# Edge products of a graph layer: from 64-row fp32 to 128-row fp32r with stacked high and low parts

## The chip, the cores and the metric

The kernel runs on one NeuronCore of a Trainium2 chip. The metric is the device time of one execution in microseconds (us). A second kind of execution is profiled: it gives a span (first to last instruction) and the trace from which all rows below are copied.

## The reference, cut to what matters

```
src, dst = edge_index                      # 131072 edges, sorted by dst; 8192 nodes, 256 channels
ea  = edge_attr @ w_e + b_e                # (131072, 64) @ (64, 256)
msg = relu(x[src] + ea)
agg = segment_sum(msg, dst, 8192)
t   = x + agg
h_local = bn1(relu(t @ w1 + b1) @ w2 + b2 + x)
# 32 blocks of 256 nodes, attention with 4 heads inside graphs of 32 nodes
h_attn  = bn2(softmax(q k^T / 8) v @ out_w.T + out_b + x)
out = h_local + h_attn
out = bn3(out + relu(out @ m_w1 + m_b1) @ m_w2 + m_b2)
return layernorm(x + out)
```

All of it is in fp32. The part that changes is the first product, `edge_attr @ w_e`.

## The kernel before, in words

**Tiles.** The edges are cut into 128 groups of 1024 edges, a group into 8 tiles of 128 edges, and two tiles make a pair: 512 pairs. A pair fills one PSUM bank of 128x512 values (128 edges, twice 256 channels). Four banks `EA[0..3]` take the pairs in turn.

**Turns.** All engines run one list of turns, written out by hand, each engine in its own program order with semaphores between them. A turn handles two pairs: turn t works on pairs 2t and 2t+1, so 256 turns carry edges and 19 more finish the nodes. A group is two turns. For one pair:

- GpSimd (POOL) issues two indirect DMAs (line 304), one per tile, which fetch the rows `x[src]` into one of 8 slots `xg`. It may be 8 pairs ahead of the engine that empties the slots.
- The pair's bank is seeded with these rows. For pairs 0 to 79 (`XB_PAIR` = 80) VectorE adds `b_e` while it seeds (`seed`, line 442). For the others `b_e` is in the rows already: VectorE adds it to all of `x` in 16 parts (`XB`) during the first turns (`add_be`, line 541), SyncE stores each part to `xb_dram`, and the later gathers read from there. ScalarE then only copies (`seed`, line 330). Seeds are made one turn ahead of the product.
- TensorE adds the edge product on top of the seed (`products`, line 707): for the two pairs of a turn four fp32 products of 64 rows. The edge attributes `ea` of one pair lie in SBUF partitions 0 to 63 and those of the other in 64 to 127, the weights `we` are there twice, so two such products use the two halves of the array at once.
- ScalarE takes the relu and rounds it to fp32r (`mh`, line 334), VectorE computes what the rounding lost (`ml`, `low`, line 533), and once per group TensorE sums both by destination with 16 fp32r products of a one-hot matrix (line 722). VectorE makes the one-hot (line 545). ScalarE copies the sum (line 339), TensorE transposes it (line 731), VectorE adds it to `aggT` (line 563).

**Nodes.** Every 8 turns a block of 256 nodes goes through attention (16 steps) and another through the layers behind it (13 steps, `node`), spread over the turns between the edge work; line 677 is the helper that issues most of their fp32 products.

**Order on the queues that the change touches.** SyncE loads `ea` into three buffers (line 201), two groups ahead of use, and waits for the product before it reuses a buffer. In every odd turn up to 31 it waits for `add_be` of a part, stores that part (line 242) and loads the next one (line 231); the parts have two buffers `xrow`. On VectorE a turn reads: seeds, then in even turns `add_agg`, `add_be` and the one-hot, then the two `low`, then attention and node steps. On ScalarE: seeds, the two `high`, in odd turns the copy of the sum, then attention and node steps.

## Time and profile before

| | us |
|---|---|
| median of three runs | 1360.22 (1359.91 to 1360.58) |
| the profiled execution | 1364.96 |
| its span | 1363.1 |
| TensorE busy | 1270.4 (93%) |
| VectorE busy | 904.9 (66%) |
| ScalarE busy | 751.6 (55%) |
| GpSimd busy | 987.6 (72%) |
| TensorE's granted clock, mean over the span | 0.979 of full speed |

Busy is a union over the span and says nothing about waits: an instruction stream can be without a gap in its issue and still show 72%. The profiled execution is longer than the median run by 4.7 us, and its span lies 1.9 us below its own time. The rows come from that one execution.

### The profile page before, as it was taken

How to read it: one execution, taken by the hardware profiler on the slowest of the kernel's cores; microseconds unless marked ns; L12 is line 12 of the kernel's file. 1: busy time of each engine (PE TensorE's matmuls, PEld its weight loads, DVE VectorE, ACT ScalarE, POOL GpSimd, SP SyncE). 2: the span in 40 equal slices, each digit the busy share in tenths (PEclk: the TensorE clock that was granted, in tenths of full speed). 3: DMA queues.
4: the chain of work that ended last, by engine and by line, in shares of the span. 5: the costliest groups of instructions: out<-in, count | busy, mean ns of one | idle time of the engine just before them, and what ended most of it. 6: DMA issues, size and time to landing. Idle time of an engine off the chain costs nothing.

```text
span 1363.1 us, 22611 instructions
## 1 busy us (share of the span) xinstructions
PE 1270.4 (93%) x8250; PEld 1024.2 (75%) x8250; DVE 904.9 (66%) x1763; ACT 751.6 (55%) x1617; POOL 987.6 (72%) x1032
## 2 busy tenths in 40 slices
PE   3787889999999999999999999999999999999997
PEld 2666678887877777777778777777877777778786
DVE  4988987666666665667666566666666666556652
ACT  1333335665665656566665666666656656565642
POOL 7777777777777777777777777777777777777710
PEclk6889999999999999999999999999999999999999
DMA  9777765555555554555555555555555555545511
GB/s 328 236 242 244 243 212 157 172 151 164 160 174 174 160 174 139 174 161 176 174 159 163 148 166 170 174 164 172 149 161 160 175 177 160 172 131 167 153 52 47
DMA packets 109648, 232.89 MB, mean 171 GB/s; under 512 B 21984, under 2 KB 46816, under 8 KB 109536
## 3 DMA queue, kind: packets, MB, share of 16 engines
q0 software_dynamic: 49152, 134.28, 34.1%
q1 hardware_dynamic: 58944, 93.87, 20.6%
q10 hardware_dynamic: 1440, 3.29, 0.6%
q8 instruction: 65, 1.06, 0.3%
q14 instruction: 47, 0.39, 0.1%
HBM read 206.19 MB, written 25.17 MB: 170 GB/s over the span
## 4 chain that ended last, share of the span: by engine, by line
POOL 35%; PE 23%; DMA 15%; issue 13%; ACT 7%; DVE 6%; SPq 0%; DVEq 0%; ACTq 0%
POOL xg L304 35%; DMA xg<-xb_dram,srcs 12%; PE both L677 8%; PE bank L722 4%; PE bank L707 4%; ACT bank L330 3%; PE bank L677 3%; ACT mh L334 2%; DVE onehot L545 1%; DMA aggT<-in_xT_dram 1%; DVE ml L533 1%; PE bank L731 1%; PE both L853 1%; DMA xg<-in_x_dram,srcs 1%; PE bank L800 1%
## 5 line engine op out<-in xcount | busy, mean ns | idle before, releaser
L304 POOL DMA_INDIRECT xg<-xb_dram,srcs x864 | 819.3, 948 | 263.2 <-issue 227.0
L330 ACT COPY bank<-xg 128x512 f32<-128x512 f32 x432 | 256.3, 598 | 373.5 <-DMA xg<-xb_dram,srcs 341.7
L533 DVE SCALAR_TENSOR_TENSOR ml<-bank,mh 128x512 fp32r<-128x512 f32 x512 | 328.6, 683 | 154.6 <-ACT mh L334 153.6
L334 ACT ACTIVATE mh<-bank 128x512 fp32r<-128x512 f32 x512 | 276.7, 593 | 137.6 <-PE bank L707 136.4
L707 PE MATMUL bank<-we,ea 64*128 64x256 f32 x2048 | 296.1, 409 | 56.7 <-DVE bank L442 28.3
L707 PEld LDWEIGHTS bank<-we,ea 64*128 64x128 f32 x2048 | 181.7, 191 | 139.1 <-issue 68.3
L722 PE MATMUL bank<-mh,onehot 128*128 128x256 f32 x1024 | 265.8, 297 | 8.3 <-DVE onehot L545 8.2
L722 PE MATMUL bank<-ml,onehot 128*128 128x256 f32 x1024 | 252.3, 284 | 0.0
L722 PEld LDWEIGHTS bank<-mh,onehot 128*128 128x128 f32 x1024 | 196.4, 192 | 51.8 <-issue 29.5
L304 POOL DMA_INDIRECT xg<-in_x_dram,srcs x160 | 167.3, 1046 | 50.8 <-issue 46.9
L722 PEld LDWEIGHTS bank<-ml,onehot 128*128 128x128 f32 x1024 | 197.1, 192 | 0.0
L563 DVE TENSOR_TENSOR aggT<-bank,aggT 128x256 f32 x128 | 54.3, 424 | 159.2 <-PE bank L731 157.5
L545 DVE TENSOR_TENSOR onehot<-bank,rel 128x1024 fp32r<-128x1024 f32 x128 | 155.4, 1214 | 0.0
L677 PE MATMUL both<-xT,iwT 128*128 128x256 f32 x512 | 124.3, 386 | 0.0
L677 PE MATMUL both<-m,h 128*128 128x256 f32 x496 | 117.5, 380 | 1.0 <-ACT h L343 1.0
L677 PEld LDWEIGHTS both<-xT,iwT 128*128 128x128 f32 x512 | 92.1, 190 | 15.2 <-issue 5.3
L677 PEld LDWEIGHTS both<-m,h 128*128 128x128 f32 x496 | 89.4, 190 | 11.2 <-issue 1.4
L339 ACT COPY agg<-bank 128x256 f32<-128x256 f32 x128 | 47.7, 373 | 54.3 <-PE bank L722 54.2
L677 PE MATMUL both<-iwT,xT 128*128 128x256 f32 x256 | 68.3, 390 | 0.3 <-DVE dif L578 0.3
L677 PE MATMUL bank<-oT,owT 128*128 128x256 f32 x256 | 65.8, 379 | 0.8 <-ACT oT L367 0.8
L677 PE MATMUL bank<-h,w 128*128 128x256 f32 x256 | 65.7, 379 | 0.0
L677 PE MATMUL bank<-o,m 128*128 128x256 f32 x264 | 62.4, 379 | 1.0 <-DVE o L606 1.0
(100 smaller groups left out, 1368.3 us busy)
## 6 DMA issues: line engine op xcount, KB each, us to landing
ea<-in_ea_dram SPq DMA_DIRECT2D x128, 256.0 KB, 5.0
xg<-xb_dram,srcs POOLq DMA_INDIRECT x864, 3.0
xT<-in_xT_dram SPq DMA_DIRECT2D x32, 256.0 KB, 3.2
aggT<-in_xT_dram SPq DMA_DIRECT2D x32, 256.0 KB, 3.9
xrow<-in_x_dram SPq DMA_DIRECT2D x16, 512.0 KB, 6.1
xb_dram<-xrow SPq DMA_DIRECT2D x16, 512.0 KB, 3.7
oT_dram<-oT SPq DMA_DIRECT2D x32, 256.0 KB, 2.3
xn<-in_x_dram SPq DMA_DIRECT2D x32, 256.0 KB, 4.5
```

Source lines behind the costliest of these rows:

```text
L304: pool.indirect_dma_start(xg[:, q % NX, n * C:(n + 1) * C], None, t["x"] if q < XB_PAIR else k.xb_dram[:, :], bass.IndirectOffsetOnAxis(k. ...
L330: nc.scalar.copy(EA[q % 4][:, :], xg[:, q % NX, :]).then_inc(s_seed, 1)
L334: nc.scalar.activation(mh[:, q % NM, :], EA[q % 4][:, :], ACT.Relu).then_inc(s_mh, 1)
L339: nc.scalar.copy(k.agg[:, :], G[:, 0:C]).then_inc(s_agg, 1)
L533: nc.vector.scalar_tensor_tensor(ml[:, q % NM, :], EA[q % 4][:, :], 0.0, mh[:, q % NM, :].bitcast(fp32), ALU.max, ALU.subtract).then_inc(s ...
L545: nc.vector.tensor_tensor(onehot[:, n % 2, :, :], G[:, 2 * P:3 * P].unsqueeze(1).to_broadcast([P, TG, P]), k.rel[:, n, :].unsqueeze(2).to_ ...
L563: nc.vector.tensor_tensor(window, G[:, 0:C].rearrange("p (c n) -> p c n", n=P), window, ALU.add).then_inc(s_added, 1)
L677: ins = nc.tensor.matmul(to, stationary(c), moving(c), start=start and c == 0, stop=stop and c == blocks - 1)
L707: ins = nc.tensor.matmul(EA[(2 * d + pair) % 4][:, two * C:(two + 1) * C], ea[rows, n % NEA, at:at + P], k.we[rows, :], start=False, stop= ...
L722: ins = nc.tensor.matmul(G[:, 0:C], onehot[:, n % 2, tile, :], half[:, q % NM, two * C:(two + 1) * C], start=tile == 0 and half is mh, sto ...
L731: ins = nc.tensor.transpose(G[:, c * P:(c + 1) * P], k.agg[:, c * P:(c + 1) * P], ident[:, :])
L800: ins = nc.tensor.matmul(X[1][at:at + DH, col:col + P], k.vn[:, b, h * DH:(h + 1) * DH], k.probT[:, H * (h % 2) + 2 * b + h // 2, :], star ...
```

## The change

Each 128x512 tile of edge attributes is split into a high part (rounded to fp32r) and a low part (what the rounding lost), and the two are stacked over 128 partitions in a new tile `eahl`: for the first pair of a product high in partitions 0 to 63 and low in 64 to 127, for the second the other way round. The weights are split the same way (`weh`, `wel`). A turn then has 8 fp32r products of 128 rows, each with 256 columns, in place of four fp32 products of 64 rows.

The split is made once per group, in odd turns. ScalarE writes the rounded tile into a bank of pairs (`EA[2]`, free between `low` of its pair and its next seed), and copies the two 64-partition halves rounded into `eahl`; VectorE subtracts the bank from `ea` in two instructions of 64x512. ScalarE's split stands behind a wait for `low` of the turn's first pair, and its copy of the group sum (`copy_agg`) now stands behind that wait too. The next seed of the bank waits for VectorE's split.

The table with `b_e` is made in 32 parts of half the size, one in every turn up to 31, and not in 16. `XB_PAIR` stays at 80. `ea` has two buffers, not three, and is loaded one turn earlier relative to its split. In the attention `ex` and `prob` now share the memory of `dif`.

```diff
-NEA = 3
+NEA = 2
-XB = 16
+XB = 32
-XB_PAIR = XB * PG + 16
+XB_PAIR = 2 * XB + 16
...
@@ sync
             def load_ea(n):
                 if n >= NEA:
-                    sp.wait_ge(s_prod, 2 * (n - NEA) + 2)
+                    sp.wait_ge(s_eah, n - NEA + 1)
+                    sp.wait_ge(s_eal, n - NEA + 1)
...
-                if turn % 2 == 1 and turn // 2 + 2 < NG:
-                    load_ea(turn // 2 + 2)
-                m = turn // 2
-                if turn % 2 == 1 and m < XB:
+                if turn == 0:
+                    load_ea(2)
+                if turn % 2 == 0 and turn // 2 + 3 < NG:
+                    load_ea(turn // 2 + 3)
+                m = turn
+                if m < XB:
                     sp.wait_ge(s_xadd, m + 1)
                     sp.dma_start(xb_parts[m, :, :, :], k.xrow[:, m % 2, :, :]
                                  ).then_inc(s_xbst[m % 2], 16)
-                if turn % 2 == 1 and 2 <= m + 1 < XB:
+                if 2 <= m + 1 < XB:
                     load_part(m + 1)
@@ scalar
+                if q % 4 == 2 and q // 4 + 2 <= NG:
+                    act.wait_ge(s_eal, q // 4 + 2)
                 nc.scalar.copy(EA[q % 4][:, :], xg[:, q % NX, :]).then_inc(s_seed, 1)
...
+            def round_ea(n, bank):
+                act.wait_ge(s_ea[n % NEA], 16 * (n // NEA + 1))
+                nc.scalar.copy(bank[:, :].bitcast(f32r), ea[:, n % NEA, :]).then_inc(s_eab, 1)
+
+            def high_ea(n):
+                nc.scalar.copy(eahl[0:ED, n % 2, 0, :], ea[0:ED, n % NEA, :])
+                nc.scalar.copy(eahl[ED:P, n % 2, 1, :], ea[ED:P, n % NEA, :]).then_inc(s_eah, 1)
...
+                n = (turn + 3) // 2
+                if turn % 2 == 1 and n < NG:
+                    act.wait_ge(s_ml, a + 1)
+                    round_ea(n, EA[a % 4])
                 if turn % 2 == 1 and 3 <= turn <= 2 * NG + 1:
                     copy_agg(turn // 2 - 1)
-                n = turn // 2 + 1
-                if turn % 2 == 0 and EA_PE <= n < NG:
-                    act.wait_ge(s_ea[n % NEA], 16 * (n // NEA + 1))
+                if turn % 2 == 1 and n < NG:
+                    high_ea(n)
@@ vector
+            def low_ea(n, bank):
+                dve.wait_ge(s_eab, n + 1)
+                nc.vector.tensor_tensor(eahl[ED:P, n % 2, 0, :], ea[0:ED, n % NEA, :],
+                                        bank[0:ED, :], ALU.subtract)
+                nc.vector.tensor_tensor(eahl[0:ED, n % 2, 1, :], ea[ED:P, n % NEA, :],
+                                        bank[ED:P, :], ALU.subtract).then_inc(s_eal, 1)
...
-                    if n < XB:
-                        add_be(n)
                     if n < NG:
                         make_onehot(n)
+                if 1 <= turn < XB:
+                    add_be(turn)
                 for q in (a, b):
                     if q < NP:
                         low(q)
+                if turn % 2 == 1 and (turn + 3) // 2 < NG:
+                    low_ea((turn + 3) // 2, EA[a % 4])
@@ tensor, products
-                for two in range(2):
-                    for pair in range(2):
-                        rows = slice(pair * ED, (pair + 1) * ED)
-                        ins = nc.tensor.matmul(EA[(2 * d + pair) % 4][:, two * C:(two + 1) * C],
-                                               ea[rows, n % NEA, at:at + P], k.we[rows, :],
+                for pair in range(2):
+                    for two in range(2):
+                        for half in (k.weh, k.wel):
+                            ins = nc.tensor.matmul(EA[(2 * d + pair) % 4][:, two * C:(two + 1) * C],
+                                                   eahl[:, n % 2, pair, at:at + P], half[:, :],
```

On VectorE, two turns of the first thirty (an odd and an even one) read in the kernel before like this; `ml<-bank,mh` is `low`, `bank<-be_rows,xg` is `seed`:

```order
L442 TENSOR_TENSOR bank<-be_rows,xg 128x512 x2
L533 SCALAR_TENSOR_TENSOR ml<-bank,mh 128x512 x2
L442 TENSOR_TENSOR bank<-be_rows,xg 128x512 x2
L552 TENSOR_LOAD base_i
L552 ISA x2
L563 ISA
L563 TENSOR_TENSOR aggT<-bank,aggT 128x2x128
L541 TENSOR_TENSOR xrow<-be_rows,xrow 128x1024
L545 TENSOR_TENSOR onehot<-bank,rel 128x1024
L533 SCALAR_TENSOR_TENSOR ml<-bank,mh 128x512 x2
```

and in the changed kernel like this (`eahl<-ea,bank` is `low_ea`):

```order
L473 TENSOR_TENSOR bank<-be_rows,xg 128x512 x2
L583 TENSOR_TENSOR xrow<-be_rows,xrow 128x512
L575 SCALAR_TENSOR_TENSOR ml<-bank,mh 128x512 x2
L481 TENSOR_TENSOR eahl<-ea,bank 64x512
L483 TENSOR_TENSOR eahl<-ea,bank 64x512
L473 TENSOR_TENSOR bank<-be_rows,xg 128x512 x2
L594 TENSOR_LOAD base_i
L594 ISA x2
L605 ISA
L605 TENSOR_TENSOR aggT<-bank,aggT 128x2x128
L587 TENSOR_TENSOR onehot<-bank,rel 128x1024
L583 TENSOR_TENSOR xrow<-be_rows,xrow 128x512
```

Two instructions of 64x512 come into every odd turn, `add_be` stands in both turns with half the length, and in the even one it has moved behind the one-hot.

On SyncE's queue, four turns of the same part of the program before:

```order
L242 DMA xb_dram<-xrow 128x1024
L231 DMA xrow<-in_x_dram 128x1024
L201 DMA ea<-in_ea_dram 128x512
L242 DMA xb_dram<-xrow 128x1024
L231 DMA xrow<-in_x_dram 128x1024
```

and in the changed kernel:

```order
L208 DMA ea<-in_ea_dram 128x512
L251 DMA xb_dram<-xrow 128x512
L238 DMA xrow<-in_x_dram 128x512
L251 DMA xb_dram<-xrow 128x512
L238 DMA xrow<-in_x_dram 128x512
L208 DMA ea<-in_ea_dram 128x512
```

A store and a load of a part now stand in every turn. The load of part m+1 stands, as before, behind the store of part m, which waits for `add_be` of part m; between that wait and `add_be` of part m+1 lies one turn, where two lay before.

## Rows read from the trace of the kernel before

**Rows 1.** What engines waited for over the whole span: us in total, times, longest.

```profile
ACT bank L330 <- DMA xg<-xb_dram,srcs: 341.7, 213, 4.5
POOL xg L304 <- issue: 273.9, 899, 0.3
...
POOL xg L304 <- DVE bank L442: 2.4, 5, 1.2
```

**Rows 2.** The page's part 5: gathers (busy, mean ns | idle before).

```profile
L304 POOL DMA_INDIRECT xg<-xb_dram,srcs x864 | 819.3, 948 | 263.2 <-issue 227.0
...
L304 POOL DMA_INDIRECT xg<-in_x_dram,srcs x160 | 167.3, 1046 | 50.8 <-issue 46.9
```

**Rows 3.** Windows by engine, busy us (instructions), PEclk, DMA share, GB/s.

```profile
27.20:97.80 70.60, 54.85 (x330) 42.30 (x332) 63.83 (x111) 21.43 (x45) 54.41 (x51) 0.80 0.73 240
97.80:183.20 85.40, 72.25 (x478) 57.33 (x478) 77.11 (x132) 30.58 (x68) 66.25 (x63) 0.98 0.75 241
...
400.00:600.00 200.00, 194.37 (x1281) 156.72 (x1280) 129.09 (x256) 123.08 (x266) 151.35 (x160) 1.00 0.55 165
```

**Rows 4.** Timeline in steady state: start, us, engine, instruction [idle before <-releaser].

```profile
606.76 1.13 PE L707 MATMUL bank<-we,ea 64*128 64x256 f32 x8
...
607.83 0.39 PE L722 MATMUL bank<-mh,onehot 128*128 128x256 f32 x1
...
609.72 0.28 PE L722 MATMUL bank<-ml,onehot 128*128 128x256 f32 x1
```

**Rows 5.** Groups by line, whole span, of VectorE and ScalarE.

```profile
L533 DVE SCALAR_TENSOR_TENSOR ml<-bank,mh 128x512 fp32r<-128x512 f32 x512 | 328.6, 683 | 154.6 <-ACT mh L334 153.6
...
L330 ACT COPY bank<-xg 128x512 f32<-128x512 f32 x432 | 256.3, 598 | 373.5 <-DMA xg<-xb_dram,srcs 341.7 <-DVE ml L533 29.1
...
L442 DVE TENSOR_TENSOR bank<-be_rows,xg 128x512 f32<-128x512 f32 x80 | 52.2, 693 | 12.9 <-DMA xg<-in_x_dram,srcs 12.7
...
L541 DVE TENSOR_TENSOR xrow<-be_rows,xrow 128x1024 f32<-128x1024 f32 x16 | 19.4, 1214 | 7.5 <-DMA xrow<-in_x_dram 7.5
```

**Rows 6.** Timeline of VectorE in the first turns.

```profile
97.78 1.23 DVE L541 TENSOR_TENSOR xrow<-be_rows,xrow 128x1024 f32<-128x1024 f32 x1 [0.42 <-DMA xrow<-in_x_dram]
98.92 1.22 DVE L545 TENSOR_TENSOR onehot<-bank,rel 128x1024 fp32r<-128x1024 f32 x1
...
116.92 1.29 DVE L533 SCALAR_TENSOR_TENSOR ml<-bank,mh 128x512 fp32r<-128x512 f32 x2
118.13 1.29 DVE L442 TENSOR_TENSOR bank<-be_rows,xg 128x512 f32<-128x512 f32 x2
119.33 0.42 DVE L563 TENSOR_TENSOR aggT<-bank,aggT 128x256 f32 x1
```

**Rows 7.** Windows of line 304 alone: gathers issued.

```profile
0.00:183.20 183.20, 139.06 (x132) 0.87 0.77 256
```

**Rows 8.** Windows of line 442 alone: seeds made.

```profile
0.00:183.20 183.20, 41.91 (x64) 0.87 0.77 256
```

**Rows 9.** DMA issues in 27.2 to 183.2: count, KB, median us to landing.

```profile
xb_dram<-xrow SPq DMA_DIRECT2D x15, 512.0 KB, 3.7
xrow<-in_x_dram SPq DMA_DIRECT2D x14, 512.0 KB, 6.1
ea<-in_ea_dram SPq DMA_DIRECT2D x15, 256.0 KB, 6.0
...
oT_dram<-oT SPq DMA_DIRECT2D x3, 256.0 KB, 2.0
```

**Rows 10.** The same view in 400 to 600.

```profile
xT<-in_xT_dram SPq DMA_DIRECT2D x5, 256.0 KB, 3.3
```

**Rows 11.** The chain of waits in the first 50 us: start, us, what.

```profile
21.11 6.03 DMA xrow<-in_x_dram
```

**Rows 12.** Timeline of GpSimd in the first turns.

```profile
98.05 1.78 POOL L304 DMA_INDIRECT xg<-in_x_dram,srcs  x1 [0.30 <-issue]
```

**Rows 13.** Timeline of TensorE near the end.

```profile
1273.83 2.08 PE L707 MATMUL bank<-we,ea 64*128 64x256 f32 x8 [2.60 <-ACT bank L330]
```

More of the change, by code:

```diff
@@ L95, in gnn_layer @@
         k.rel = sb("rel", [P, NG, TG])
-        k.we = sb("we", [P, C])
+        k.weh, k.wel = sb("weh", [P, C], f32r), sb("wel", [P, C], f32r)
         k.be_rows = sb("be_rows", [P, C])
@@ L122, in gnn_layer @@
         k.dst_p = k.oT[:, :, :, :].rearrange("p a c (g t) -> p (a c g) t", t=TG).bitcast(i32)
+        k.we = k.qT[:, 0, :]
         k.gammas = k.xn[:, :, :, :].rearrange("p a b c -> p (a b) c")[:, 0:3, :]
@@ L160, in program @@
         s_oh = sem("s_onehot_made")
+        s_weh, s_wel = sem("s_we_high"), sem("s_we_low")
+        s_eab, s_eah, s_eal = (sem(n) for n in ("s_ea_high_in_bank", "s_ea_high", "s_ea_low"))
         s_pre = [sem(f"s_agg_preloaded_{n}") for n in range(2)]
@@ L401, in node @@
                                          ).then_inc(s_root, 1)
+            act.wait_ge(s_we, 16)
+            nc.scalar.copy(k.weh[:, :], k.we[:, :]).then_inc(s_weh, 1)
+            for n in range(2):
+                round_ea(n, X[1 + n])
+                high_ea(n)
             for turn in range(TURNS):
@@ L441, in seed @@
                     dve.wait_ge(s_ml, q - 3)
+                if q % 4 == 2 and q >= 6:
+                    dve.wait_ge(s_eal, q // 4 + 2)
                 nc.vector.tensor_tensor(
@@ L455, in _ @@
             seed(1)
+            dve.wait_ge(s_weh, 1)
+            nc.vector.tensor_tensor(k.wel[:, :], k.we[:, :], k.weh[:, :].bitcast(fp32),
+                                    ALU.subtract).then_inc(s_wel, 1)
+            low_ea(0, X[1])
             dve.wait_ge(s_dstg, 16)
@@ L643, in node @@
                     ins.then_inc(s_y, 1)
+            low_ea(1, X[2])
             add_be(0)
@@ L690, in _ @@
                                 ).then_inc(s_baseT, 1)
-            pe.wait_ge(s_we, 16)
+            pe.wait_ge(s_wel, 1)
             def products(d):
                 n, h = d // 2, d % 2
-                if h == 0 and n < EA_PE:
-                    pe.wait_ge(s_ea[n % NEA], 16 * (n // NEA + 1))
+                if h == 0 and n < 2:
+                    pe.wait_ge(s_eah, n + 1)
+                    pe.wait_ge(s_eal, n + 1)
                 if 2 * d < XB_PAIR:
```

17 lines of the change are left out of this document (8 added, 9 removed).

## The prediction

> **What bounds the kernel now.** I read the waits first. GpSimd never waits for anybody for long: before nearly every gather it sits idle 0.3 us on its own issue, and in the whole span it waits 2.4 us for VectorE's seeds [rows 1]. ScalarE, in contrast, waits 341.7 us for gathered rows, and TensorE, busy 97% of a steady stretch, still gets its pauses from late seeds [rows 1, 3, 13]. So the stream of gathers sets the pace, although the page calls GpSimd 72% busy. Its price: (819.3 + 263.2) / 864 = 1.253 us for one late gather, (167.3 + 50.8) / 160 = 1.363 us for one of the first 160 [rows 2]. Four gathers make a turn: 5.01 us later, 5.45 us in the first 40 turns.
>
> The first gathers are slower because some are stretched from 0.95 us to as much as 1.78 us, and these lie beside `add_be` and the seeds of VectorE, which read two SBUF operands: the 1.78 us gather at 98.05 runs beside the `add_be` at 97.78 [rows 6, 12]. The Trainium skill says the same in GPSIMD Engine Reference, Key points: GpSimd contends with VectorE instructions that have two SBUF inputs. By that rule the new `low_ea`, one operand of which is in PSUM, stretches nothing; `low`, which reads PSUM too, runs all through the stretch 400 to 600, where 160 gathers were busy 151.35 us, 0.946 us each [rows 3, 5].
>
> Then I look at who is close behind GpSimd, by stretch. From 400 to 600 VectorE is busy 129.09 of 200 us and ScalarE 123.08. From 27.2 to 183.2, which is turns 0 to 30 (turn 30 has made seeds number 63 and 64 by 183.2), VectorE is busy 63.83 + 77.11 = 140.9 of 156.0 us, 90% [rows 3, 8]. A turn takes 5.20 us there. At 183.2 GpSimd has issued 132 gathers, 66 pairs, against 64 pairs seeded [rows 7, 8]: it is 2 pairs ahead where the slots allow 8. That unused lead decides what a slower VectorE costs.
>
> **TensorE.** Products before: from the start of one to the next instruction on TensorE 607.83 - 606.76 = 1.07 us [rows 4]. The new ones have the form of the one-hot sums: fp32r, 128 rows, 256 columns. Sixteen of these start from 607.83 to 609.72, 0.126 us apart [rows 4]. Eight make 1.01 us, or 0.95 us if the first longer step is not paid. I take a gain of 0.1 us a turn. Bounds: none, and, if a gap of 64-row work at both ends of the products goes, 0.3 us. Because GpSimd sets the pace it counts only where TensorE is the chain, from the last wait for a seed at 1273.83 to the end [rows 13]: some 7 turns with products, -1 us.
>
> The Trainium skill, TensorEngine Tiling (Array Packing), Key Properties, says that a change of tiling mode drains TensorE. The 1.07 us would leave 0.1 us for it, but no row isolates the drain. If the rule alone were right and TensorE the bound, the change would be worth the gain of every turn; that is the last rival.
>
> **ScalarE.** It adds per group one copy into PSUM (598 ns as line 330's) and two copies of 64x512. For the last two no row exists; length along the free dimension is that of line 330, so I take 0.6 us; bounds 0.37 us and 0.7 us [rows 5]. Sum 1.8 us per group, 0.9 us a turn, on an engine busy 123.08/200 x 5.01 = 3.1 us a turn: 4.0 of 5.01 us. In the first turns it is far from full. It costs nothing as throughput. As latency: in odd turns the next seeds stand behind the wait for `low`, the rounding, the copy of the sum and two more copies. Counted from the end of an odd turn's products that is 1.1 (two `high`) + 0.2 + 0.6 + 0.4 + 1.1 + about 1 of node work = 4.4 us and then 1.1 us of seeds, against more than 8 us until the product that needs them. The one tight place is a short turn behind an attention step, where eight instructions of 256 elements (8 x 0.42 = 3.4 us, by the 128x256 one at 119.33) stand ahead of `low` on VectorE; I estimate a stall up to 0.5 us per 8 turns, inside the 5.6 us that TensorE is idle in 200 us [rows 3] plus the 4 us that it gains. So: nothing.
>
> **VectorE.** `low_ea` is two instructions of 64x512 with a PSUM operand per group. The row nearest is `low`: 683 ns, two in 118.13 - 116.92 = 1.21 us, 0.60 us each in a stream [rows 5, 6]. Bounds 0.42 us (the 128x256 instruction at 119.33) and 0.69 us. That is 0.60 us a turn. `add_be`: 1.14 us before per two turns (97.78 to 98.92), now two of the seeds' size, 1.20 us: +0.03 a turn. The first `low_ea` waits a little for ScalarE's bank: +0.07. Sum +0.70 us a turn.
>
> Behind turn 32 this is covered (0.65 + 129.09/200 x 5.01 = 3.9 of 5.01 us). In turns 0 to 30 the cover is 10%. Pace without gathers: (156.0 - 3)/30 + 0.70 = 5.80 us; the 3 us are my estimate of what VectorE waited there for gathers, out of the 12.7 us in all [rows 5]. If all its idle time there vanished, 140.9/30 + 0.70 = 5.40 us. What GpSimd tolerates: the gather of pair 66 needs pair 58 seeded, the work of turn 28, by 183.2. The first part now has 256 KB, not 512, and its load landed at 27.14 [rows 11]; I let it land 2.5 us sooner, so turn 0 starts at 24.7 and the limit is (183.2 - 24.7)/28 = 5.66 us a turn. At 5.80 turn 28 comes at 187.1: 3.9 us late, and four more turns against GpSimd's 85.40/63 x 4 = 5.42 us add 1.5. Together +5.4 us. Bounds: 0 (5.40) and +10.
>
> **SyncE and the parts.** Before, between `add_be` of part m and that of part m+1 there were two turns; the load landed after 6.1 us at the median and only 0.42 us was waited for one at 97.78 [rows 6, 9]. Now it is one turn, and the load is issued behind the store, 0.40 us after `add_be`. From an even turn's `add_be` to the next one VectorE has two `low` and two seeds, 2.4 us, plus the attention or node steps of that turn (about 3 us in two of four cases, none to 1.3 in the other two, counted at 0.42 us an instruction). From an odd one it has 2.4 + 1.2 + 0.35 + 1.14 = 5.1 us. Landing time of 256 KB: lower bound 3.3 us [rows 10], upper 6.0 [rows 9]. I take 4.0: a store of 256 KB lands in 2.0 (oT's row), and 512 KB behind a store of 512 KB land 6.1 + 0.4 - 3.7 = 2.8 us after it, so half needs 1.4, with 0.6 us for gathers and `ea` in between. Then 4.4 us are needed, and the bare turns wait 2.0 us, two in eight in turns 1 to 16, and 1.3 and 0.5 in the 16 behind them with node work: 8 + 3.6 = 11.6 us, of which some 4 lie in idle time counted already. +8 us. At 3.3 us: +2. At 6.0 us nearly every turn waits, some 14 us in eight turns: +50.
>
> **Sum.** The stages add: +5.4 + 8 (early) - 1 (end) - 1 (two half-length `add_be` hold off a gather for less time than one: squares of the lengths, 32 x 0.69^2 = 15 against 16 x 1.21^2 = 23, beside 67 for the 40 double seeds, of the 160 x 0.11 = 18 us that the first gathers are stretched) = +11 us. The profiled execution, span 1363.1 in 1364.96 us, would be 1376. The median of the runs stands 4.7 us under it; the difference carries over: 1360.2 + 11 = 1371 us.
>
> **Rivals.**
> - The lead covers it. VectorE's idle time shrinks, loads land in 3.3 us, the pace stays under 5.66 us. Then only savings are left: GpSimd's 1.2 us wait (the longest in rows 1) for a late first seed, 1.6 us less stretching, 1 us at the end: 1356.4, faster. For it: 6 unused pairs, worth 6 x 2.6 = 16 us. Against: VectorE at 90%. It decides from a pace below 5.66 us. With part of the delay left: up to 1363.
> - Latency in steady state. If ScalarE's order costs TensorE over 1.1 + 0.8 us in 8 turns (its idle time and gain there), TensorE with its waits becomes slower than 40.1 us in 8 turns. At 1.5 us over, 27 times, +40: 1400. For it: TensorE at 97%, with six steps put between `high` and the next seeds. Against: seeds a turn ahead, eight slots.
> - The parts' loads take 6 us: +50, with the +5 partly inside: about 1412.
> - TensorE is the bound after all: 256 x 0.11 = 28 us, 1332. Against it: GpSimd without a pause.
>
> **Chances.** Forecast 0.48 (its own range 1363.5 to 1390); covered 0.27, of it 0.12 faster and 0.15 the same; latency 0.14; slow loads 0.08; TensorE 0.03. A measurement of this kernel can tell about 0.2%, 2.7 us. Faster 0.15, same 0.15, slower 0.70. The range 1357 to 1404 leaves out TensorE's case, the fastest end of the covered one, and the slow loads.
>
> **What would show it.** Right: gathers of line 304 among the first 160 that wait for the seed by VectorE, tens of us and not 2.4; VectorE over 93% busy from 25 to 200 us and turn 30 at some 205 us, not 183; waits of `add_be` for `xrow`, 5 to 15 us in all; from 400 to 600 still 160 gathers; eight products at 0.12 us steps. Wrong: gathers fewer than 160 in that stretch (latency), no wait of GpSimd in the first 200 us (covered), or a last gather at 1302 with an end elsewhere.

## The result, and the profile after

The changed kernel takes 1390.67 us (median of 4 runs, 1387.56 to 1392.12), the kernel before 1360.31 us (4 runs, 1359.91 to 1360.58): 1.022 times as long, interval 1.0203 to 1.0238, +30.4 us. The forecast was 1371, +11, with a range of 1357 to 1404. Its direction and the place of the loss hold; its size is a third of what came. The step that failed is the sum for VectorE's early stage, +13.4 us with the parts' loads, where the runs show 26.0: VectorE fell behind faster, above all by its waits for the parts, and the gathers' lead took up less of it.

| | before | after |
|---|---|---|
| span of the profiled execution, us | 1363.1 | 1389.1 |
| first 160 gathers, busy + idle, us | 218.1 | 242.3 |
| other 864 gathers, busy + idle, us | 1082.5 | 1083.7 |
| start of the last gather, us | 1301.58 | 1326.87 |
| from there to the end of the span, us | 61.5 | 62.2 |
| seeds of turn 32 start, us | 192.73 | 225.82 |
| first gather from the finished table, us | 220.27 | 246.23 |

The groups of gathers after (busy, mean ns of one | idle before) come first, to be held against [rows 2]:

```profile
L313 POOL DMA_INDIRECT xg<-xb_dram,srcs x864 | 818.6, 947 | 265.1 <-issue 241.0 <-ACT bank L341 22.0 <-DVE bank L473 2.1
L313 POOL DMA_INDIRECT xg<-in_x_dram,srcs x160 | 161.0, 1006 | 81.3 <-issue 42.7 <-DVE bank L473 37.1 <-DMA srcs<-in_srcs_dram 1.5
```

Of the 26.0 us between the spans, 24.2 lie in the first 160 gathers, and there in idle time alone, 81.3 against 50.8 us; the gathers themselves became shorter. Another 1.8 us are the idle time in front of the 161st gather (2.09 against 0.30 us), which still waits for a seed of VectorE. The rest of the kernel adds nothing. What ended the idle time stands in the waits (total us, times, longest), which answer to [rows 1]:

```profile
POOL xg L313 <- issue: 283.7, 931, 0.3
ACT bank L352 <- DVE ml L575: 212.7, 126, 6.5
...
POOL xg L313 <- DVE bank L473: 39.2, 20, 3.5
PE both L722 <- ACT h L364: 38.5, 30, 1.6
...
DVE xrow L583 <- DMA xrow<-in_x_dram: 19.0, 9, 3.5
```

GpSimd waits for VectorE's seeds 39.2 us in 20 pieces, where it waited 2.4. ScalarE no longer waits for gathered rows (341.7 us before); its longest waits are now in front of the copy of line 352 (`round_ea`), which needs `low` to be done with the bank. The waits of GpSimd in its timeline (start, us, instruction, idle before it):

```profile
30.04 1.14 POOL L313 DMA_INDIRECT xg<-in_x_dram,srcs  x1 [1.31 <-DVE bank L473]
...
71.41 1.15 POOL L313 DMA_INDIRECT xg<-in_x_dram,srcs  x1 [3.21 <-DVE bank L473]
...
120.20 1.14 POOL L313 DMA_INDIRECT xg<-in_x_dram,srcs  x1 [3.47 <-DVE bank L473]
...
246.23 0.94 POOL L313 DMA_INDIRECT xg<-xb_dram,srcs  x1 [2.09 <-DVE bank L473]
```

They run from the first turn to the 161st gather, 246.23, and there is none of this size behind it. The windows by engine, PE, PEld, DVE, ACT, POOL (instructions), show both stages, to be held against [rows 3]:

```profile
27.20:225.80 198.60, 142.05 (x851) 124.92 (x852) 175.72 (x306) 80.91 (x165) 129.94 (x128) 0.86 0.67 208
400.00:600.00 200.00, 187.92 (x1290) 172.22 (x1289) 158.17 (x297) 159.71 (x329) 151.23 (x161) 1.00 0.57 166
```

From 400 to 600 there are 161 gathers in 151.23 us, as before (160 in 151.35), although VectorE and ScalarE are now busy 158 and 160 of 200 us. But the chain of work that ended last, in part 4 of the page, no longer runs through them. Before it read:

```profile
POOL 35%; PE 23%; DMA 15%; issue 13%; ACT 7%; DVE 6%; SPq 0%; DVEq 0%; ACTq 0%
```

and after:

```profile
PE 45%; DVE 32%; ACT 13%; DMA 4%; issue 3%; DVEq 1%; SPq 0%; ACTq 0%
```

No seed that ScalarE makes waits for its rows any more. ScalarE starts the seed of pair 144 (counted from 0) at 422.31 us and that of pair 464 at 1216.85, which is 4.97 us a turn, where the gathers take 5.01. So behind the table TensorE, VectorE and ScalarE run at a pace of their own, only 0.04 us a turn faster than the gathers. This small margin matters for the size of the loss. The 161st gather waits for the first seed of turn 35. Before, VectorE started it at 209.55, and the gather started 10.0 us after the seed's end:

```profile
209.55 1.29 DVE L442 TENSOR_TENSOR bank<-be_rows,xg 128x512 f32<-128x512 f32 x2
...
220.27 1.47 POOL L304 DMA_INDIRECT xg<-xb_dram,srcs  x1 [0.30 <-issue]
```

In the changed kernel VectorE comes to it 35.2 us later:

```profile
244.75 1.29 DVE L473 TENSOR_TENSOR bank<-be_rows,xg 128x512 f32<-128x512 f32 x2
```

and the gather starts at 246.23, 26.0 us later than before. The lead of the gathers took up 9.2 us of VectorE's lateness, and the engines behind them make these 9 us good at 0.04 us a turn over the 220 turns that are left. By this reckoning the kernel would have ended up to 9 us later without that margin.

In the first stretch VectorE is busy 175.72 of 198.6 us. Its timeline shows what fills a turn there:

```profile
95.49 0.69 DVE L583 TENSOR_TENSOR xrow<-be_rows,xrow 128x512 f32<-128x512 f32 x1 [1.79 <-DMA xrow<-in_x_dram]
96.10 1.28 DVE L575 SCALAR_TENSOR_TENSOR ml<-bank,mh 128x512 fp32r<-128x512 f32 x2
97.44 0.68 DVE L481 TENSOR_TENSOR eahl<-ea,bank 64x512 fp32r<-64x512 f32 x1
98.14 0.69 DVE L483 TENSOR_TENSOR eahl<-ea,bank 64x512 fp32r<-64x512 f32 x1
98.96 1.30 DVE L473 TENSOR_TENSOR bank<-be_rows,xg 128x512 f32<-128x512 f32 x2
```

The `add_be` at 95.49 sits idle 1.79 us for its part. The second `low` starts some 0.6 us after the first and would be followed at about 97.30; the first low half starts at 97.44, and from there to the seeds are 98.96 - 97.44 = 1.52 us. With the 0.14 us before it, `low_ea` takes 1.66 us of these two turns. The chain of waits (start, us, what) shows where the part was late:

```profile
41.24 0.61 DVE xrow L583
41.85 0.02 issue
41.86 0.33 SPq L251
...
42.23 5.12 DMA xrow<-in_x_dram
...
47.38 0.69 DVE xrow L583
```

It is a ring: `add_be` lets SyncE store the part (0.33 us of issue), the next load goes out behind the store, at 42.23, and the following `add_be` starts as the load lands, 5.12 us later. With 16 parts the ring had two turns for one round, with 32 it has one.

On TensorE the eight products (start and duration, us) went as forecast:

```profile
602.14 0.36 PE L753 MATMUL bank<-weh,eahl 128*128 128x256 f32 x1
602.34 0.28 PE L753 MATMUL bank<-wel,eahl 128*128 128x256 f32 x1
602.46 0.28 PE L753 MATMUL bank<-weh,eahl 128*128 128x256 f32 x1
...
603.18 0.28 PE L767 MATMUL bank<-mh,onehot 128*128 128x256 f32 x1
```

From the first product to the next instruction are 603.18 - 602.14 = 1.04 us, 1.07 before [rows 4]. Its busy time from 400 to 600 fell from 194.37 to 187.92 us, and the gathers' pace didn't change with it.

### The profile page after: what moved, and what is told of

It is laid out like the page before. It is cut to its first block, busy times and chain, and to the rows that moved or that the text cites. A ratio compares the mean times of both kernels' runs of the same rounds, so it can differ in the third digit from the quotient of the medians.

```text
span 1389.1 us, 23482 instructions
## 1 busy us (share of the span) xinstructions
PE 1234.5 (89%) x8250; PEld 1123.0 (81%) x8250; DVE 1088.4 (78%) x2036; ACT 973.5 (70%) x2002; POOL 980.6 (71%) x1032
## 4 chain that ended last, share of the span: by engine, by line
PE 45%; DVE 32%; ACT 13%; DMA 4%; issue 3%; DVEq 1%; SPq 0%; ACTq 0%
PE both L722 16%; DVE ml L575 9%; PE bank L722 8%; PE bank L767 8%; PE bank L753 8%; DVE probT L637 4%; DVE dif L620 4%; DVE mx L616 4%; DVE onehot L587 4%; DMA xrow<-in_x_dram 3%; ACT bank L352 3%; ACT eahl L356 2%; PE bank L845 2%; ACT bank L341 2%; ACT eahl L355 2%
## 5 line engine op out<-in xcount | busy, mean ns | idle before, releaser
L753 PE MATMUL bank<-weh,eahl 128*128 128x256 f32 x1024 | 302.3, 327 | 26.6 <-DVE bank L473 26.6
L341 ACT COPY bank<-xg 128x512 f32<-128x512 f32 x432 | 245.2, 601 | 31.1 <-DVE ml L575 29.5
L753 PE MATMUL bank<-wel,eahl 128*128 128x256 f32 x1024 | 260.9, 286 | 0.0
L767 PE MATMUL bank<-mh,onehot 128*128 128x256 f32 x1024 | 257.8, 288 | 1.1 <-DVE onehot L587 1.1
L753 PEld LDWEIGHTS bank<-weh,eahl 128*128 128x128 f32 x1024 | 198.7, 194 | 40.7 <-DVE bank L473 31.3
L352 ACT CAST bank<-ea 128x512 fp32r<-128x512 f32 x127 | 75.0, 590 | 212.7 <-DVE ml L575 212.7
L313 POOL DMA_INDIRECT xg<-in_x_dram,srcs x160 | 161.0, 1006 | 81.3 <-issue 42.7
L753 PEld LDWEIGHTS bank<-wel,eahl 128*128 128x128 f32 x1024 | 199.7, 195 | 4.6
L776 PE MATMUL bank<-ident,agg 128*128 128x128 f32 x256 | 51.6, 284 | 51.7 <-ACT agg L360 51.7
L481 DVE TENSOR_TENSOR eahl<-ea,bank 64x512 fp32r<-64x512 f32 x127 | 86.5, 681 | 7.6
L483 DVE TENSOR_TENSOR eahl<-ea,bank 64x512 fp32r<-64x512 f32 x127 | 87.6, 690 | 1.8
```

The costliest lines, as they stand in the source:

```text
L313: pool.indirect_dma_start(xg[:, q % NX, n * C:(n + 1) * C], None, t["x"] if q < XB_PAIR else k.xb_dram[:, :], bass.IndirectOffsetOnAxis(k. ...
L341: nc.scalar.copy(EA[q % 4][:, :], xg[:, q % NX, :]).then_inc(s_seed, 1)
L352: nc.scalar.copy(bank[:, :].bitcast(f32r), ea[:, n % NEA, :]).then_inc(s_eab, 1)
L481: nc.vector.tensor_tensor(eahl[ED:P, n % 2, 0, :], ea[0:ED, n % NEA, :], bank[0:ED, :], ALU.subtract)
L483: nc.vector.tensor_tensor(eahl[0:ED, n % 2, 1, :], ea[ED:P, n % NEA, :], bank[ED:P, :], ALU.subtract).then_inc(s_eal, 1)
L753: ins = nc.tensor.matmul(EA[(2 * d + pair) % 4][:, two * C:(two + 1) * C], eahl[:, n % 2, pair, at:at + P], half[:, :], start=False, stop= ...
```

## The experiments

A job is a set of runs made one after the other on one chip, the kernel before among them. Two kinds have to be told apart. In the jobs that ran the full-length variants, the kernel before itself took 1766 to 1800 us (medians); in the jobs with the lightened kernels (below) it took 1359 to 1360, as at first, and one chip showed both, in two jobs one after the other. In the long jobs the gathers don't set the pace:

```profile
400.00:600.00 200.00, 160.56 (x927) 126.54 (x927) 94.99 (x186) 90.89 (x191) 111.54 (x118) 0.90 0.42 124
```

This is the kernel before in such a job (the same columns as in the windows above): 118 gathers in 200 us instead of 160, and TensorE only 160.56 us busy. The waits of the same run:

```profile
ACT mh L334 <- remote: 443.7, 73, 13.7
POOL xg L304 <- ACT bank L330: 388.5, 110, 5.8
...
PEld bank L707 <- issue: 95.5, 210, 4.0
PEld bank L722 <- issue: 73.4, 131, 6.1
```

In the rows shown TensorE's weight loads pause for nothing that the profile shows, up to 6.1 us at once. Such rows stood in the first profile too, but smaller: 68.3 us in all on line 707 (the longest 4.0 as here), and 29.5 us with none over 0.3 on line 722. A wait whose releaser the profile can't name is "remote"; ScalarE has 443.7 us of them on one line, and had none. The granted clock is 0.90 in this stretch, against 1.00; whether that comes from the pauses or has a part in them isn't separated. A loss of 30 us in the stream of gathers can't be read there. The cause of these jobs is open.

**Full variants in long jobs.** Four edits, each run in two or more jobs. b32, the kernel before with the table in 32 parts alone:

```diff
-XB = 16
+XB = 32
...
-                if turn % 2 == 1 and m < XB:
+                if m < XB:
...
-                    if n < XB:
-                        add_be(n)
...
+                if 1 <= turn < XB:
+                    add_be(turn)
```

> The kernel before with one part of the change alone: the table in 32 parts of half the size, one add_be per turn, XB_PAIR still 80. Theory (VectorE's early work uses up the gathers' lead): about 15 us of add_be waiting for xrow as in the changed kernel, turn 32 at 205 to 212 us, which the lead of 6 unused pairs nearly covers: 1360 to 1366 us. Rival (the loads of the parts alone are the loss): 1375 us or more. Rival (the parts cost nothing, all loss is the split): 1359 to 1361 us with waits of add_be under 5 us.

> The same kernel as b32 (the 32 parts alone in the kernel before). Theory: about 15 us of add_be waiting for xrow, nearly covered by the gathers' lead: 1360 to 1366 us. Rival (the parts are the loss): 1375 us or more.

nosplit, the changed kernel without the split beyond groups 0 and 1 (the products take the old halves, so the edge part of the result is that of the first groups). The waits that belong to these calls go or are bounded with them:

```diff
-                    round_ea(n, EA[a % 4])
...
-                    high_ea(n)
...
-                    low_ea((turn + 3) // 2, EA[a % 4])
```

> The changed kernel with the split of the edge attributes left out for all groups but the first two (eahl keeps the first two groups' values, so the edge products are computed from those): TensorE's new products and the 32 parts remain, ScalarE and VectorE do none of the split. Theory: as b32 less at most 2 us, 1358 to 1365 us: TensorE's gain per turn buys nothing in the steady stretch, where still 160 gathers fall in 200 us, and ScalarE waits for gathers again. Rival (TensorE sets the pace): 1335 to 1345 us.

> The same kernel as nosplit (new products and parts, no split but for the first two groups, so the edge products use old values). Theory: 1358 to 1365 us, ScalarE waits for gathers again, 160 gathers in 400 to 600 us. Rival (TensorE sets the pace): 1335 to 1345 us.

nolow, the same with ScalarE's half of the split kept (only the low halves are the old ones); the seeds that waited for `low_ea` wait for `round_ea` instead:

```diff
-                if turn % 2 == 1 and (turn + 3) // 2 < NG:
-                    low_ea((turn + 3) // 2, EA[a % 4])
```

> The changed kernel with VectorE's half of the split (low_ea) left out for all groups but the first two; ScalarE's rounding into the bank and its two copies remain, with their places in the order. The low halves of the edge attributes keep old values. Theory: VectorE's early pace is that of b32, so 1358 to 1366 us, within 3 us of nosplit. Rival (ScalarE's order and latency cost in the steady stretch): most of the loss stays, 1380 us or more, with fewer than 160 gathers in 400 to 600 us.

> The same kernel as nolow (ScalarE's part of the split stays, VectorE's is left out but for the first two groups, so the low halves keep old values). Theory: within 3 us of nosplit, 1358 to 1366 us. Rival (ScalarE's order costs in the steady stretch): 1380 us or more; on the slow chip nolow was as slow as pf and 1.2% above nosplit, which speaks for this rival where TensorE is the bound.

pf, the changed kernel with the load of the next part ahead of SyncE's wait:

```diff
                 m = turn
+                if 2 <= m + 1 < XB:
+                    load_part(m + 1)
                 if m < XB:
                     sp.wait_ge(s_xadd, m + 1)
...
-                if 2 <= m + 1 < XB:
-                    load_part(m + 1)
```

> The changed kernel with SyncE's load of part m+1 issued ahead of its wait for add_be of part m (it waits only for the store of part m-1), nothing else changed. Theory: the 15.5 us of add_be waiting for xrow after turn 0 go almost whole, early pace 5.7 to 5.9 us a turn in place of 6.21, gathers wait 15 to 25 us for seeds in place of 39, 1374 to 1382 us. Rival (the split alone would be enough to use up the lead): 1385 to 1390 us, since VectorE then waits elsewhere. Rival (the parts' loads are the whole loss): 1360 to 1363 us.

> The same kernel as pf, for a comparison on a chip on which the kernel before takes 1360 us; on the chip of the first comparison it took 1766 us, TensorE paused between its own matmuls there and gathers waited for ScalarE, so that another bound was measured. Theory: 15 us less waiting of add_be for xrow, gathers wait 15 to 25 us for seeds, 1374 to 1382 us. Rival (the split alone uses up the lead): 1385 to 1390 us. Rival (the parts' loads are the whole loss): 1360 to 1363 us.

> The changed kernel with SyncE issuing the load of the table's part m+1 ahead of its wait for the sum of part m, so that VectorE no longer waits for a part in the early stage (19 us in the changed kernel, 3 us with this edit on the chip with TensorE's pauses). If this lands on a chip where the kernel before takes 1360 us. Theory (the loss is VectorE's pace past the lead): 10 to 16 us less than the changed kernel, so 1375 to 1381, 1.011 to 1.016 times the kernel before. Rival (the waits only cover time that VectorE would lose anyway, to late gathers): 1388 to 1391.

And both kernels themselves, with ib (run again as ib3): the kernel before with all seeds on ScalarE, and the bias added to the first 80 pairs by TensorE from its high and low parts (be2) with a constant 1/64, four products a turn:

```diff
+                            nc.tensor.matmul(EA[(2 * d + pair) % 4][:, two * C:(two + 1) * C],
+                                             k.frac[:, :], k.be2[:, :], start=False, stop=True,
+                                             skip_group_check=True)
```

> The kernel before, unchanged, for its trace on the chip at hand. If it takes 1360 us, the rows of the first trace again: 160 gathers in 400 to 600 us. If it takes 1766 us: about 120 gathers in 400 to 600 us, and idle time of TensorE in front of matmuls that wait for nothing, which would show that the gathers don't set the pace on that chip.

> The changed kernel itself, to have its ratio beside the others'. If the kernel before takes 1360 us here, 1.022 as before. If it takes about 1766 us, as on the chip of the two comparisons so far, no theory fixes the ratio: TensorE pauses between its own instructions there and the gathers are not the bound. If the loss is bound to the gathers' lead in the first 230 us, the ratio is the one of pf (1.013 to 1.015) within 0.4%; if the parts' late loads cost there too, 15 us or 0.9% more.

> The kernel before with the seeds of the first 80 pairs moved from VectorE to ScalarE (a plain copy, as for all later pairs) and b_e added on TensorE by one more fp32r product of 128 rows per tile (weights of 1/64, moving operand the high part of b_e in 64 rows and the low part in the other 64); the table, the parts and everything later as before. Theory: VectorE's 80 instructions with two SBUF operands were most of what stretched the first gathers, and VectorE's load of the first 40 turns falls by 1.2 us a turn, so where gathers set the pace the first 160 take about 205 us in place of 218, and the time is 1345 to 1350 us (0.99). Rival (the stretching comes from add_be, or from DMA traffic): 1358 to 1362 us. Where TensorE's own pauses set the pace: no change, or up to 19 us longer for 160 more products of 0.12 us.

> The kernel before with all seeds copied by ScalarE, and the bias of the edge rows added to the first 80 pairs' banks by TensorE (a 128-row product of a constant 1/64 with the bias' high and low parts): VectorE's reads of two SBUF operands per pair are gone and the gathers' mean is 0.97 us instead of 1.05 (measured on the chip with TensorE's pauses). If the kernel before takes 1360 us here. Theory (the first 160 gathers are worth what they take, one for one): 8 to 14 us less than the kernel before, 1346 to 1352, since ScalarE's seeds leave no wait of the gathers. Rival (ScalarE, with eight more columns of work a turn, or TensorE's 8 added products a turn, set the pace in their place): 1360 or more.

| | median us (times the kernel before, interval) |
|---|---|
| b32 | 1768.22 (1.0004, 0.9962 to 1.0045); 1770.19 (1.0011, 0.9983 to 1.0039) |
| nosplit | 1767.42 (1.0015, 0.9955 to 1.0075); 1770.79 (0.9997, 0.9968 to 1.0027) |
| nolow | 1789.79 (1.013, 1.0088 to 1.0173); 1786.14 (1.010, 1.0062 to 1.0138) |
| pf | 1789.51 (1.013, 1.0082 to 1.0178); 1790.44 (1.0149, 1.006 to 1.0238); 1795.29 (1.0121, 1.0052 to 1.019) |
| kernel after | 1804.5 (1.0042, 1.0004 to 1.0079) |
| kernel before, one run | 1803.34 |
| ib | 1802.07 (1.0004, 0.9965 to 1.0043); 1766.16 (1.0018, 0.9985 to 1.005) |

The times expected of b32, nosplit, nolow and pf, and most of those of ib, were for a kernel before of 1360 us, so these runs don't test them. before_here came as expected for a long job (118 gathers), and so did ib (no change). after_again didn't: the changed kernel costs 1.004 here, not 1.022, and less than the 1.013 to 1.015 of pf that were expected of it within 0.4%. nolow and pf, which leave out something of it, show 1.010 to 1.015 in other jobs, and nosplit and b32 show nothing; so in these jobs the cost goes with ScalarE's part of the split, perhaps, and not with VectorE's. With TensorE's pauses unexplained I don't build on that. Two rows of early turns can be used, since they are of one engine and its load. pf brought VectorE's wait for its parts down:

```profile
DVE xrow L583 <- DMA xrow<-in_x_dram: 3.0, 1, 3.0
```

And ib, without VectorE's reads of two SBUF operands in the seeds, has somewhat shorter gathers in the first 160:

```profile
L304 POOL DMA_INDIRECT xg<-in_x_dram,srcs x160 | 155.5, 972 | 115.3 <-ACT bank L333 63.7 <-issue 50.0 <-DMA srcs<-in_srcs_dram 1.6
```

972 ns is the mean (977 in ib3). It has to be held against the kernel before in the same job, which has 1003, and not against the 1046 of [rows 2]: the difference is 31 ns. Whether that is worth time where the gathers set the pace was not shown: both runs of ib fell into long jobs.

**Lightened kernels.** To take TensorE out of the question, four kernels and later a fifth leave out a part of its work, all in the same way: of each node-side product only the first block of the contraction is computed, the products with z are left out, and of the sums over a group the low halves.

```diff
-                for c in range(blocks):
...
+                for c in range(1):
...
-                    for half in (mh, ml):
+                    for half in (mh,):
```

The diff is cut; the products with z go in a third place. Waits, order and the other engines' work stay. light_before and light_after are the two kernels so lightened, light_b32, light_nolow and light_pf the variants above.

> The kernel before, with TensorE lightened: it leaves out every block but the first of the node side's products, the products with z, and the low halves in the sums over a group. On this chip the kernel before takes 1766 to 1803 us because TensorE pauses between its own matmuls; with some 0.9 us a turn less of them, by 1.25 us a gather the last of 1024 gathers should end at about 1300 and the kernel take 1350 to 1370 us. If the pauses grow with something else than the count of matmuls, it stays over 1600. Early stage as in the profile of the kernel before: some 145 gathers issued by 200 us.

> The changed kernel lightened in the same way. My theory (the loss is made in the first 160 gathers, by VectorE's turn of 6.2 us with the low halves and the 32 parts' loads): light_before plus 20 to 33 us, all of it in the first 160 gathers, whose busy and idle time together is some 24 us more than in light_before. Rival (the loss is made by the 128-row products or the bank lent for the split, over the whole kernel): the difference is spread over the 1024 gathers. Rival (the loss belongs to TensorE and is gone when it is lightened): within 3 us of light_before.

> light_before with the table in 32 parts alone (80 pairs seeded on VectorE as before). Theory: the loads of the parts make VectorE wait some 15 us in the first 160 gathers, but the lead of the gathers (16 us at turn 32) takes that up: light_before plus 0 to 4 us. Rival (the parts' loads alone are the loss): plus 15 to 20 us.

> light_after without VectorE's low halves beyond the first two groups (the low halves of those are used again): ScalarE's half of the split, the 128-row products and the 32 parts stay. Theory: VectorE's turn falls by 0.83 us, 32 turns of that are 27 us, so nearly all the loss is gone: light_before plus 0 to 6 us. Rival (loads, bank or products make it): light_before plus 15 us or more.

> light_after with the load of part m+1 issued ahead of SyncE's wait for the sum of part m. On a chip where the kernel before takes 1360 us: light_after is 1363.0 us and light_before 1338.0. Theory (the waits for the parts' loads are on VectorE's path once the lead is used up): VectorE's waits for xrow fall from 17 us to under 6, and the first 160 gathers' busy and idle time from 237.4 to some 225, so 1349 to 1355 us, near light_nolow's 1345. Rival (a wait gone is only replaced by a wait for a late gather): 1360 to 1364. On a chip with TensorE's pauses only the wait for xrow (under 6 us) can be read from it.

| | median us (runs) | over light_before | first 160 gathers, busy + idle, us | over light_before |
|---|---|---|---|---|
| light_before | 1337.98 (1337.06 to 1338.37) | | 214.2 | |
| light_b32 | 1344.93 (1341.92 to 1349.59) | +6.9 | 219.7 | +5.5 |
| light_nolow | 1345.19 (1344.48 to 1347.17) | +7.2 | 221.8 | +7.6 |
| light_pf | 1347.67 (1347.05 to 1348.78) | +9.7 | 223.5 | +9.3 |
| light_after | 1363.00 (1361.53 to 1365.47) | +25.0 | 237.4 | +23.2 |

Against the kernel before of their jobs (1359.72 and 1359.16 us) the ratios are 0.9838 (0.9822 to 0.9854), 0.99 (0.9877 to 0.9922), 0.9895 (0.9878 to 0.9911), 0.9914 (0.9897 to 0.993) and 1.0021 (1.0011 to 1.003). light_pf ran in a job of its own, on another chip; the two jobs' times of the kernel before differ by 0.6 us. light_after came as expected. The expectation of light_before was 1350 to 1370; it was shorter, since a lighter TensorE also shortens the stretch behind the last gather's start, to 39.0 us from 61.5. light_b32 and light_nolow were expected to cost 4 and 6 us at most and cost 6.9 and 7.2, and light_pf was expected at 1349 to 1355 and came 1.3 us below.

The rows of the gathers, in the order light_before, light_after:

```profile
L304 POOL DMA_INDIRECT xg<-in_x_dram,srcs x160 | 163.4, 1021 | 50.8 <-issue 46.3 <-DVE bank L442 3.0 <-DMA srcs<-in_srcs_dram 1.5
```

```profile
L313 POOL DMA_INDIRECT xg<-xb_dram,srcs x864 | 819.4, 948 | 263.2 <-issue 239.7 <-ACT bank L341 23.2 <-DVE bank L473 0.3
L313 POOL DMA_INDIRECT xg<-in_x_dram,srcs x160 | 161.1, 1007 | 76.3 <-issue 43.9 <-DVE bank L473 31.0 <-DMA srcs<-in_srcs_dram 1.4
```

The idle time of the 864 late gathers is 263.2 us in all five kernels. A loss of 25.0 us is there with a TensorE that has a quarter less to do, and nearly all of it in the first 160 gathers. That settles it against two rivals: the loss doesn't belong to TensorE's products, and it isn't spread over the kernel by the lent bank. light_b32 and light_nolow, which differ in the new products, in ScalarE's half of the split and in the lent bank, are 0.3 us apart: here these three cost next to nothing. One thing the light kernels don't show is the full kernel's small margin behind the table. In light_after ScalarE comes back to the gathers at 4.73 us a turn between the seeds of pairs 80 and 144 and then waits for rows again; in the full kernel it is 4.97 us.

What VectorE waits for its parts, and GpSimd for VectorE, stands in the waits of light_b32, light_nolow, light_pf and light_after, one fence each:

```profile
DVE xrow L541 <- DMA xrow<-in_x_dram: 28.7, 21, 5.8
POOL xg L304 <- DVE bank L442: 10.5, 7, 3.2
```

```profile
DVE xrow L583 <- DMA xrow<-in_x_dram: 24.5, 22, 3.8
POOL xg L313 <- DVE bank L473: 13.7, 13, 2.4
```

```profile
POOL xg L313 <- DVE bank L473: 13.9, 11, 2.6
...
DVE xrow L583 <- DMA xrow<-in_x_dram: 3.2, 1, 3.2
```

```profile
POOL xg L313 <- DVE bank L473: 31.4, 16, 3.2
...
DVE xrow L583 <- DMA xrow<-in_x_dram: 16.9, 8, 2.8
```

Removing the low halves takes 17.8 us off the median, removing the waits for the parts takes 15.3 us off, and each of the two burdens alone costs 7 to 10 us. They add as burdens, not as losses. The traces show it at the seed that the 161st gather waits for, the first of turn 35. light_before starts it at 203.63 us; light_b32, light_nolow, light_pf and light_after start it 13.9, 16.5, 19.0 and 32.9 us later, and their 161st gather starts 5.5, 7.5, 9.3 and 23.2 us later. In all four 8.4 to 9.7 us of VectorE's lateness vanish in the gathers' lead, as 9.2 us do in the full kernels, and every us beyond is paid. That two burdens together cost more than the sum of their single costs (25.0 against 6.9 or 7.2 + 9.7) is this lead counted once and not twice.

A wait is no fixed burden either. Without the low halves VectorE waits longer for its parts, 24.5 us instead of 16.9, since it comes to `add_be` sooner and the loads don't.

light_pf also says what the ring costs: the edit moves one issue, and it takes back 15.3 of the 25.0 us. The landing time from issue fell with it, at the median from 4.3 to 3.4 us (27.2 to 183.2 us); that this is because the load no longer stands behind the store is argued, not shown.

## Why the prediction was right and where it failed

**The bound, right for the kernel before, and only just for the changed one.** The gathers set the pace before, and the loss arises where GpSimd has to wait. From 400 to 600 there are 161 of them, and the new work of the other engines doesn't slow them. But the forecast counted on gathers that still hold up the others behind the table. In the changed kernel no seed there waits for rows and the last chain has no gather in it; that the end came as late as the gathers did, 26.0 us, rests on the 0.04 us a turn by which the other engines are faster. TensorE's term (-1 at the end) didn't come: the stretch behind the last gather's start is 62.2 us, 61.5 before.

**ScalarE as throughput, right; as latency, right with luck.** It is busy 159.71 of 200 us, 4.0 us a turn as summed. The 864 late gathers take 1.2 us more, and 1.8 us of wait in front of their first one belong to the early stage. But the pace of 4.97 us a turn against 5.01 means that the forecast's "nothing" held by 0.3 us in 8 turns. Which of the three engines sets the 4.97 us isn't separated; with the lighter TensorE it was 4.73.

**The direction, right.** VectorE in the first stretch, its low halves and the parts' loads; light_nolow and light_pf show both.

**The size of the early stage, wrong: the step that failed.** The forecast lets +5.4 us for VectorE's pace and +8 for the parts' loads be lost, 13.4 in all; measured are 26.0 at the 161st gather. Its pace (5.80 us a turn and 8 us of waits over 32 turns) puts turn 32 at 24.7 + 32 x 5.80 + 8 = 218.3 us, and it came at 225.82; it puts turn 35 at 24.7 + 35 x 5.80 + 8 = 235.7, and it came at 244.75. So 9.1 of the missing 12.6 us are VectorE's pace. In busy and idle time up to turn 32 the forecast is made up of four terms, and the traces have all four (windows from 27.2 us to 192.7 before and to 225.8 after):

| VectorE up to the seeds of turn 32, against before | forecast, us | measured, us |
|---|---|---|
| start of turn 0 | -2.5 | 0 |
| more busy time | 32 x 0.70 = +22.4 | 175.72 - 150.26 = +25.46 |
| more waits for parts, behind the first | +8 | 15.47 - 0.42 = +15.05 |
| other idle time | -2.3 | 7.41 - 14.82 = -7.41 |
| sum | +25.6 | +33.10 |

- The start. I let the first part of 256 KB land 2.5 us sooner. `add_be` started at 27.21, as before:

```profile
27.21 0.69 DVE L583 TENSOR_TENSOR xrow<-be_rows,xrow 128x512 f32<-128x512 f32 x1 [3.53 <-DMA xrow<-in_x_dram]
```

 The smaller part landed 5.21 us after its issue and not 6.03, but the issue came at 21.98 us and not at 21.11. Nothing was left of the gain.
- `low_ea`. I took 0.60 us each in a stream, from two `low`, and 0.07 for the bank, 0.67 a turn. In the turns shown it is 1.66 us in two turns, 0.83: the two take 0.70 and 0.82 us from start to start, and do not overlap the next as two `low` do. My upper bound, 0.69, was the better row.
- The parts' loads. This is the term with the largest error, 7.1 us. I counted 11.6 us of waits and took 4 of them as idle time counted already. In the profile they are 19.0 us, 3.53 of them at the start: 15.5. The landing took 4.3 us at the median, against 4.0 in the sum, but 5.12 and more for some.
- The idle time. VectorE had more of it to give than I took, by 5.1 us, and that hid part of the rest.

The other 3.5 us are the lead. The forecast has turn 35 26.1 us later than before and lets 13.4 of that be lost, so it counts on a lead that takes up 12.7 us (its covered rival even on 16). The measured one took up 9.2. I had read it at turn 28, where the gather started 13.7 us after the end of the seed it needs (183.5 us in the trace); in front of the 161st gather it was 10.0.

**VectorE's share, wrong.** I wanted over 93% busy in the early stage as a sign. It is 175.72 / 198.6 = 88% up to turn 32. With the 15.5 us of waits for parts it is 96%: a wait in the engine's own stream fills it as work does, and the sign should have been the sum.

**The stretch term, wrong.** The first 160 gathers did become shorter, 161.0 against 167.3 us, but where VectorE sets the pace, a shorter gather only waits longer. Nor is it shown that the smaller `add_be` shorten them: light_before has 163.4 us, light_b32 161.4 and light_pf 163.0. The contention itself shows in the trace of the kernel before. Of its first 160 gathers, the 80 that run beside an `add_be` or a seed of VectorE for more than 0.1 us take 1.14 us on the mean, and the 66 that meet none take 0.95. The Trainium skill states in GPSIMD Engine Reference, Key points, that GpSimd contends with VectorE instructions that have two SBUF inputs. These two means agree with it, and so do the 1003 and 972 ns of the kernel before and ib in one job.

**The carry-over, wrong by 4.4 us (30.4 between the medians, 26.0 between the spans).** The sum was made against a profiled execution 4.7 us over its median; that of the changed kernel stands at its median (1390.78, 1390.67). light_before's first 160 gathers were busy 163.4 us where the kernel before's profile has 167.3, so some of the 4.7 us may be a loss that only that execution had. That is argued, not shown. Where the 5.4 us lie by which the full loss of 30.4 is larger than the 25.0 of the light kernels stays open too.

**The marks.** As forecast: tens of us of gathers' waits (39.2), products at 0.12 us steps, 161 gathers in the steady stretch (160). Off: turn 30 at 212.94 us (205), and waits for parts of 19.0 us in all where 5 to 15 were forecast (15.5 without the first). The rival in which the lead covers it failed: even one part of the change alone cost 7 us in the light kernels. The rival of latency showed none of its signs, but it had only the 0.3 us in 8 turns to go.

**Open.** The cause of the long jobs, and the costs of nolow and pf in them; ib where the gathers set the pace; pf and nolow at full length there, since only their light versions ran in short jobs; what sets the 4.97 us. No version was shown to beat the kernel before.

## What to carry to other kernels

A lead of one engine over another is a reserve that all edits in the stage share. Add their burdens first, take the reserve off once, and read the reserve at the last item of the stage. Two edits that cost 7 and 10 us alone cost 25 together here.

Look also at how much faster the engines behind the stream are than the stream itself. A lateness that the lead hides has to be made good there, and the changed kernel could do so by only 0.04 us a turn.

When the parts of a buffer ring are halved, follow one round of it (compute, store, issue, load, compute) and compare that with the time of a turn. If the load is issued behind a wait for the computation of the part before, moving it ahead is the first thing to try.

Take an added instruction's cost from its start-to-start time beside unlike neighbours, not from a stream of its own kind.

## What the runs showed of the hardware

- The same program took 1359 to 1360 us in some jobs and 1766 to 1800 us in others (medians), and one chip showed both; in the long ones TensorE's weight loads pause with no releaser in the profile, up to 6.1 us in the rows shown. A comparison needs the kernel before in the same job.
- Two 64x512 VectorE instructions with a PSUM operand take 0.68 and 0.69 us, as long as 128x512 ones (0.69), and start 0.70 us apart, against 0.60 for two `low`: half the partitions saved nothing.
- Eight 128-row products of fp32r take 1.04 us where four 64-row fp32 products, eight instructions in the trace, took 1.07.
- An indirect gather took 0.95 us and 0.30 us of issue, and 1.14 us on the mean beside VectorE instructions with two SBUF operands.
